# Six PSUM banks for two rings of score tiles: four and two in place of three and three

## What is computed

```python
attn = einsum('bhql,bkl->bhqk', q_lat, c_kv) / sqrt(hs)   # 16 heads, hs = 8, latent 64
attn = softmax(where(causal, attn, -inf))
y    = einsum('bhqk,bkl->bhql', attn, c_kv) -> einsum with v_eff, reshape to (T, C)
x    = layernorm(x + y)
# experts: 8, of 512 hidden, top 2, capacity 80, in 2 groups of 1024 tokens
x    = layernorm(x + combine(expert(dispatch(x))))
```

## Time and profile before

| what | value |
|---|---|
| median of 3 runs | 586.45 us (584.77 to 587.04) |
| profiled execution, its own time | 584.08 us |
| its span, first to last instruction | 582.3 us |
| TensorE / VectorE / ScalarE / GpSimd busy | 521.1 / 441.9 / 349.7 / 63.1 us |
| first score tile of step 0 | 48.4 us |
| first of the last unit's steps to the last `attn_v` | about 480 to 515 us |
| matmuls for maxima, line 1070 | 640, 221.4 us |
| matmuls for exponentials, line 1090 | 640, 214.1 us |
| attention times values, line 1107 | 1280, 146.9 us |

### The profile page before, as it was taken

The page is one execution under the profiler, slowest core; times in us unless marked ns, Lnnn a source line. Parts: engine busy times, 40 slices in busy tenths (PEclk is TensorE's granted clock), DMA queues, the critical chain, the costliest instruction groups (busy, mean ns, idle before and its releaser), DMA issues.

```text
span 582.3 us, 10231 instructions
## 1 busy us (share of the span) xinstructions
PE 521.1 (89%) x3443; PEld 213.6 (37%) x3443; DVE 441.9 (76%) x1300; ACT 349.7 (60%) x719; POOL 63.1 (11%) x64
## 2 busy tenths in 40 slices
PE   4967999898999998999999989999999999955991
PEld 2523333333333333333445433333233222223891
DVE  3797999897988989889658768979888862445617
ACT  0614556656668765677756657667777779934231
POOL 9400000000000000171000036000000000000031
PEclk9956999999999999999999999999999999985997
DMA  3489994200000300011000015100000000000024
GB/s 88 123 223 208 192 262 121 49 2 2 1 2 2 82 1 2 7 51 41 2 2 12 2 33 48 6 2 0 2 2 1 2 2 10 19 11 0 1 42 55
DMA packets 25794, 24.88 MB, mean 43 GB/s; under 512 B 2827, under 2 KB 23053, under 8 KB 25741
## 3 DMA queue, kind: packets, MB, share of 16 engines
q1 hardware_dynamic: 21660, 20.42, 14.5%
q0 software_dynamic: 1280, 2.62, 3.8%
q10 hardware_dynamic: 2800, 1.18, 0.8%
HBM read 16.81 MB, written 7.28 MB: 41 GB/s over the span
## 4 chain that ended last, share of the span: by engine, by line
issue 53%; PE 32%; DVE 8%; DMA 3%; POOL 2%; ACT 1%; SPq 0%; ACTq 0%; POOLq 0%; DVEq 0%
PE ring L1070 10%; PE acc L1107 9%; PE ring L1090 7%; DVE unused L797 2%; DVE part_max L792 2%; DMA qT<-maxT 1%; PE ms L1198 1%; PE ms L1192 1%; PE ring L1094 1%; POOL back L595 1%; DMA back<-exp_out,slot_out 1%; DMA wo<-in_L_attn_W_dkv 1%; POOL res L605 1%; PE ring L1049 1%; PE ms L1141 0%
## 5 line engine op out<-in xcount | busy, mean ns | idle before, releaser
L665 ACT ACTIVATE probs<-ring 128x512 f32<-128x512 f32 (+3 forms) x560 | 270.3, 536 | 139.5 <-PE ring L1094 79.0
L792 DVE TENSOR_REDUCE part_max<-ring 128x1 f32<-128x512 f32 x384 | 254.2, 686 | 41.7 <-PE ring L1070 38.8
L1070 PE MATMUL ring<-kT,qT 126*128 126x512 bf16 (+3 forms) x640 | 221.4, 360 | 11.2 <-DVE part_max L797 5.6
L1090 PE MATMUL ring<-qT,kT 128*128 128x512 bf16 (+3 forms) x640 | 214.1, 351 | 4.1 <-DMA qT<-maxT 3.1
L1107 PE MATMUL acc<-probs,v 128*9 128x512 f32 (+3 forms) x1280 | 146.9, 531 | 0.9 <-ACT yT L676 0.9
L797 DVE CUSTOM_DVE_ANT_0 unused<-ring,causal 128x128 bf16<-128x128 f32 (+3 forms) x256 | 120.2, 483 | 17.5 <-PE ring L1070 15.9
L1070 PEld LDWEIGHTS ring<-kT,qT 126*128 126x128 bf16 x640 | 61.9, 98 | 182.5 <-DVE part_max L792 103.7
L1090 PEld LDWEIGHTS ring<-qT,kT 128*128 128x128 bf16 x640 | 61.7, 98 | 44.6 <-ACT probs L663 15.7
L1094 PE MATMUL ring<-later,ident 128*128 128x128 bf16 x256 | 55.1, 220 | 0.0
L1107 PEld LDWEIGHTS acc<-probs,v 128*9 128x9 f32 x1280 | 19.0, 88 | 50.5 <-issue 26.6
L663 ACT ACTIVATE probs<-ring 128x1024 f32<-128x1024 f32 (+3 forms) x40 | 33.2, 899 | 3.0 <-issue 1.8
(11 more groups left out here) (179 smaller groups left out, 327.6 us busy)
## 6 DMA issues: line engine op xcount, KB each, us to landing
kT<-parts_k SPq DMA_DIRECT2D x9, 384.0 KB
qT<-parts_q SPq DMA_DIRECT2D x9, 384.0 KB
wi<-in_L_ffn_wi SPq DMA_DIRECT2D x1, 2048.0 KB, 20.6
parts_k<-wi SPq DMA_DIRECT2D x3, 384.0 KB, 4.0
parts_q<-wi SPq DMA_DIRECT2D x3, 384.0 KB, 4.8
kT<-parts_k SPq DMA_DIRECT2D x12, 96.0 KB
qT<-parts_q SPq DMA_DIRECT2D x12, 96.0 KB
x<-in_L_attn_x ACTq DMA_DIRECT2D x4, 256.0 KB, 4.4
```

The costliest lines, as they stand in the source:

```text
L665: nc.scalar.activation(probs[:, at, 0:width], ring[:, bank, 0:width], ACT.Exp).then_inc(exp_done, 1)
L792: nc.vector.tensor_reduce(dst, sc[i % SRING][:, :], AX.X, ALU.max).then_inc(sc_used, 1)
L1070: nc.tensor.matmul(sc[i % SRING][:, 0:w], qT[s % 2][0:MROW, head, qt * P:(qt + 1) * P], kT[0:MROW, head, c * QUERIES:c * QUERIES + w], sta ...
L1090: ins = nc.tensor.matmul(bank[:, 0:QUERIES - off], kT[:, head, j * P:(j + 1) * P], qT[s % 2][:, head, off:QUERIES], start=True, stop=True, ...
```

## The change

`SRING` becomes 4, and a new `MRING` = 2 stands wherever the maxima's ring was meant. Banks 0 to 3 are now for the exponentials' tiles and banks 4 and 5 for the maxima's. So an item waits for the maximum two before it, and a score tile for the exponential four before it. From step 140 on the six banks are used as before. The weight products of the prologue move from `sc[2]` to `scT[3]`. The order of all instructions stays the same.

```diff
-SRING = 3
+SRING = 4
+MRING = 2
...
 def score_bank(n):
-    return n % SRING if n < HG * WIDE else n % (2 * SRING)
+    return n % SRING if n < HG * WIDE else n % (SRING + MRING)
...
 def used_before(n):
-    return max((m for m in range(max(0, n - 4 * SRING), n) if score_bank(m) == score_bank(n)), default=None)
+    return max((m for m in range(max(0, n - 2 * (SRING + MRING)), n) if score_bank(m) == score_bank(n)), default=None)
...
-        ring = ctx.enter_context(nc.psum_tensor("ring", [P, 2 * SRING, QUERIES], F32))
+        ring = ctx.enter_context(nc.psum_tensor("ring", [P, SRING + MRING, QUERIES], F32))
         scT = [ring[:, i, :] for i in range(SRING)]
-        sc = [ring[:, SRING + i, :] for i in range(SRING)]
+        sc = [ring[:, SRING + i, :] for i in range(MRING)]
...
-            nc.vector.tensor_copy(kw.rearrange("p (d h) -> p d h", h=HEADS), by_value(sc[2][:, 0:C])).then_inc(w_kept, 1)
-            nc.vector.tensor_copy(vw, sc[2][:, C:2 * C]).then_inc(w_kept, 1)
+            nc.vector.tensor_copy(kw.rearrange("p (d h) -> p d h", h=HEADS), by_value(scT[3][:, 0:C])).then_inc(w_kept, 1)
+            nc.vector.tensor_copy(vw, scT[3][:, C:2 * C]).then_inc(w_kept, 1)
...
-                if i >= SRING:
-                    pe.wait_ge(sc_used, i - SRING + 1)
+                if i >= MRING:
+                    pe.wait_ge(sc_used, i - MRING + 1)
```

More of the change, by code:

```diff
@@ L791, in row_max @@
                 if c < super_of(u):
-                    nc.vector.tensor_reduce(dst, sc[i % SRING][:, :], AX.X, ALU.max).then_inc(sc_used, 1)
+                    nc.vector.tensor_reduce(dst, sc[i % MRING][:, :], AX.X, ALU.max).then_inc(sc_used, 1)
                 else:
@@ L796, in row_max @@
                         dve.wait_ge(sc_used, i - 1)
-                    nc.vector.tensor_tensor_reduce(unused[i % 2][:, 0:w], sc[i % SRING][:, 0:w], causal[:, QUERIES - w:QUERIES], 1.0, 3 * BIG,
+                    nc.vector.tensor_tensor_reduce(unused[i % 2][:, 0:w], sc[i % MRING][:, 0:w], causal[:, QUERIES - w:QUERIES], 1.0, 3 * BIG,
                                                    ALU.add, ALU.max, dst).then_inc(sc_used, 1)
@@ L1038, in _ @@
             pe.wait_ge(w_kept, 6)
-            nc.tensor.matmul(sc[2][:, 0:C], wdkv, keffT, start=True, stop=True)
-            nc.tensor.matmul(sc[2][:, C:2 * C], wdkv, veff, start=True, stop=True).then_inc(w_made, 1)
+            nc.tensor.matmul(scT[3][:, 0:C], wdkv, keffT, start=True, stop=True)
+            nc.tensor.matmul(scT[3][:, C:2 * C], wdkv, veff, start=True, stop=True).then_inc(w_made, 1)
             pe.wait_ge(w_kept, 8)
@@ L1066, in scores_for_max @@
                     pe.wait_ge(kq_in[s], 16 * 2 * PARTS)
-                if i >= SRING:
-                    pe.wait_ge(sc_used, i - SRING + 1)
+                if i >= MRING:
+                    pe.wait_ge(sc_used, i - MRING + 1)
                 w = QUERIES if c < s else (qt + 1) * P
-                nc.tensor.matmul(sc[i % SRING][:, 0:w], qT[s % 2][0:MROW, head, qt * P:(qt + 1) * P],
+                nc.tensor.matmul(sc[i % MRING][:, 0:w], qT[s % 2][0:MROW, head, qt * P:(qt + 1) * P],
                                  kT[0:MROW, head, c * QUERIES:c * QUERIES + w], start=True, stop=True).then_inc(sc_made, 1)
```

## The result

The changed kernel takes 644.01 us in the median of 4 runs (640.02 to 644.95), against 585.61 us for the kernel before, whose runs are now four (582.73 to 587.04). The ratio is 1.100, with a 95% interval of 1.096 to 1.104. The forecast was 633 us, from 612 to 652. The profiled execution took 643.08 us, 59.0 more than that of before; its span is 641.3.

What follows compares the result with a forecast made beforehand. TensorE's single queue was taken to bound the kernel, with two maxima banks returning too late. Terms 38.7 + 1 + 6.5 + 1.5 − 0.7 = 47.0 us gave a median forecast of 633 us, range 612 to 652.

Steps and rivals of the forecast that it cites:

- A0: First maximum of the next plain step on TensorE; forecast to start 1.17 us after A2, where 0.88 was wanted.
- A1: Second maximum of the next plain step; forecast to start 1.77 us after A2, where 1.32 was wanted.
- A2: First of the last two maxima before a plain step's end; next A2 forecast after 3.27 us, before 2.82.
- Term 1: Plain steps, 16 to 138: 86 steps without other work at their end lose 0.45 us typically, 38.7 us in all.
- Term 2: Steps ending in other TensorE work: zero for 16 expert steps, 0.05 us each for 21 others; 1 us.
- Term 3: First 16 steps, up to eight items, VectorE full: 0.40 us a step in the mean, 6.5 us in all.
- Term 5: Fourth bank for the exponentials: gives back only waits that make TensorE stand, taken as −0.7 us.
- Term 4: Before step 0, the first unit's 16 items lose time to the two-bank round trip: 1.5 us, from 0 to 2.
- A3: Last maximum before a plain step's end; where it is 384 wide, the forecast cost is 0.36 us.
- rival B: Larger loss: VectorE's other work, 20 us between steps 16 and 138, lands on TensorE too; about 653 us, chance 0.10.
- Rival C: TensorE's clock falls: half of the 123 steps at half clock, 144 us more, about 777 us, chance 0.02.

Runs made afterwards that it cites:

- half-read kernels: Maxima reading half their columns, four-and-two against three-and-three banks: full maxima alone 604.84 against 572.88 us; both forms 591.63 against 568.99 us.
- the reordering: Second gap's score issued ahead of that gap's maxima: in the changed kernel 633.22 us; in the kernel before, with three and three banks, 584.41 us.
- five-bank kernel: Changed kernel with the exponentials back on three banks, maxima on two, bank 3 idle up to step 140: 640.41 us.

## Why the prediction was right, and what it sized wrong

**The mechanism was right, and the cost too low.** A bank comes back after fill, read and return, and two banks can't cover the plain step: A0 at 1.18, A1 at 1.78, period 3.30, all within 0.03 us of the working. The half-read kernels show that the price falls with the time a bank is held; the reordering shows that what stands between A2 and A1 sets the period; five banks do as six. The forecast was 633 with a range of 612 to 652; the measured value lies 11 us above the forecast. In the traces 59.0 us were lost where the sum had 47.0, and no error hid another: terms 1, 2, 3 and 5 all came out higher than worked out, and in the stretch of term 4 the trace lost 2.1 us more. The forecast's own bounds, given as 618 to 648, add up to some 651 at the upper end (term 1 at 0.55 a step, term 2 at 6, term 3 at 10).

In what follows a step is measured from its second score to the next step's second score in both traces, which puts a wait where the forecast counted it.

**Term 1, plain steps.** 38.7 us forecast for 86 steps, 41.3 measured. The working fits the single step: 0.47 us where all is full (0.45 worked out), 0.39 where A3 is 384 wide (0.36), 0.60 where three banks already bound (0.60). The 2.6 us more lie mostly before step 33, where the traces give 6.8 us for 11 such steps in place of about 4: the three of them that have six or seven items, wide and narrow in turn, grew by 0.84 to 0.99 us each.

**Term 2, steps with other work.** 1 us forecast, 3.5 measured: 1.2 in two of the 16 expert steps and 2.2 in the other 21 together, of which 11 did not grow at all and one with transposes grew by 0.7 us. The forecast had named growth in these steps as a sign of rival B. There is some, but far from the 20 us of rival B, in which all of VectorE's other work lands on TensorE.

**Term 3, the first 16 steps, was mis-sized most.** The text priced one late item at each block, 0.40 us a step and 6.5 in all. The trace gives 9.5 for these 16 steps, 0.59 each and inside the forecast's 3 to 10; the 11.0 of the table hold step 16 as well. What the text lacked is that a stall can come at every wide-narrow pair within a step, 1.17 us where the kernel before took 0.81, and not once a step.

**Term 4, before step 0.** The items cost 1.45 us by three traces, 1.5 forecast, though in the trace of the run with three banks there most of that was lost again by the end of the second unit. The profile had 2.1 us more in this stretch, which is within what profiles of kernels with three banks there differ by.

**Term 5, the fourth bank.** −0.7 us was forecast; the five-bank kernel says zero. The last step with a wait, step 139, and the tail make up the last 1.2 us.

**The clock.** The granted clock is 1.00, the upper of its two levels, in every stretch of the changed kernel from 60 to 500 us. Two of them:

```profile
120.00:150.00 30.00, 24.34 (x164) 8.67 (x164) 24.20 (x82) 15.48 (x35) 1.27 (x1) 1.00 0.01 1
455.00:480.00 25.00, 23.86 (x132) 5.03 (x124) 18.59 (x37) 16.84 (x31) 0.00 (x0) 1.00 0.00 1
```

Rival C falls. The Trainium skill, "TensorE: Matmul & The Clock Gate", section "A second HAM failure mode: psum-queue depth-cycling", warns that short idles while cycling PSUM banks make the clock swing between its levels. That did not come true for two stalls a step, of 0.30 and 0.16 us. The Trainium skill, "Perfetto Trace Analysis", section "Matmul Optimizations", asks that all eight banks be used. That did not decide anything here: eight banks split four and two took 644 us, seven took 640, and eight split three and three 585.

## What to carry to other kernels

Count a ring by its round trip: fill to read, read, signal back, and for each further bank the reader's pitch; compare that with the distances at which the filling engine wants the banks in its real order, the long blocks in that order included. The engine's idle time in the profile of a well-fed ring says nothing about how many buffers can go: 0.7 us of waits on the exponentials' ring hid that giving its third bank to the maxima cost 16 us, and behind 5.2 us before the full maxima stood a third bank worth 58. Where tile sizes mix, count the work that a buffer brings, since a narrow tile takes up a buffer as a wide one does and gives its reader less to do.

## What the runs showed that was not expected

Waits of 0.30 and 0.16 us in a step can't be read off the busy share. TensorE's went from 89% to 85% while the plain step lengthened by 17%, because a record of 0.38 us covers a queue slot of 0.22. The starts of successive matmuls show it in full. The idle time on the reading engine shows most of it: from 41.7 to 79.5 us before the full maxima and from 17.5 to 25.3 before the diagonal ones, 46 us of the 59.
